# First attention: causal masks on VectorE and GpSimd instead of as matrix products, with a new order of work

## The reference

```python
qkv = x @ Wqkv.T + bqkv                       # x normalised over its 256 values before
q, k, v = split(qkv)                          # 16 heads of 16
q = q * rope + rotate(q) * (1.0 - rope)       # same for k
att = einsum('bhtd,bhsd->bhts', q, k) / 4
att = softmax(where(tril, att, -inf), axis=-1)
y = einsum('bhts,bhsd->bhtd', att, v)
return y @ Wproj.T + bproj                    # added to x
```

## Time and profile before

| | us |
|---|---|
| three runs | 3191.21, 3200.32, 3200.8 (median 3200.32) |
| the profiled execution | 3190.54, its span 3188.8 |
| seven bodies of the first attention | 79.5 to 629.5 of the span |
| the last body | 629.5 to 705 |
| TensorE busy over the span | 2539.1 |
| VectorE, ScalarE, GpSimd busy | 1845.6, 1238.0, 983.2 |
| mean granted TensorE clock | 0.908 of 2.4 GHz |

### The profile page before, as it was taken

The page is one execution under the profiler, slowest core; times in us unless marked ns, Lnnn a source line. Parts: engine busy times, 40 slices in busy tenths (PEclk is TensorE's granted clock), DMA queues, the critical chain, the costliest instruction groups (busy, mean ns, idle before and its releaser), DMA issues. The chain is left out here.

```text
span 3188.8 us, 51896 instructions
## 1 busy us (share of the span) xinstructions
PE 2539.1 (80%) x18615; PEld 2207.7 (69%) x18615; DVE 1845.6 (58%) x3241; ACT 1238.0 (39%) x1845; POOL 983.2 (31%) x1102
## 2 busy tenths in 40 slices
PE   1988888885069999980368777785999999999999
PEld 1777667765068888880256666675788888888888
DVE  5455555545057777775597777744744544544543
ACT  0444444442034444441123333332444444444444
POOL 3444445401734444437244444451000000000000
PEclk9899999985589999995589999997999999999999
DMA  2000000003256666654354554423422222221321
GB/s 80 1 2 2 1 1 1 1 11 128 97 179 209 211 213 212 211 193 145 94 139 126 130 129 123 123 57 116 146 97 79 86 84 77 89 81 66 100 78 60
DMA packets 195231, 317.13 MB, mean 99 GB/s; under 512 B 28757, under 2 KB 103449, under 8 KB 195097
## 3 DMA queue, kind: packets, MB, share of 16 engines
q1 hardware_dynamic: 182856, 277.00, 28.9%
q0 software_dynamic: 12240, 38.28, 3.5%
HBM read 274.83 MB, written 40.37 MB: 99 GB/s over the span
## 5 line engine op out<-in xcount | busy, mean ns | idle before, releaser
L2015 DVE TENSOR_TENSOR e_h_lo<-e_h,e_h_hi 128x512 fp32r<-128x512 f32 x320 | 221.6, 692 | 481.2 <-ACT e_h_hi L2081 481.0
L2068 ACT ACTIVATE e_h<-e_h_ps,e_b 128x512 f32<-128x512 f32 x320 | 220.3, 688 | 491.7 <-PE e_h_ps L2132 461.1
L2146 PE MATMUL e_y_ps<-e_w_hi,e_h_hi 128*128 128x256 f32 x1280 | 366.3, 286 | 22.8 <-DVE e_h_lo L2015 22.7
L2146 PE MATMUL e_y_ps<-e_w_hi,e_h_lo 128*128 128x256 f32 x1280 | 361.7, 283 | 0.0
L2146 PE MATMUL e_y_ps<-e_w_lo,e_h_hi 128*128 128x256 f32 x1280 | 361.5, 282 | 0.0
L1028 POOL TENSOR_TENSOR e_w_lo<-e_w,e_w_hi 128x2048 fp32r<-128x2048 f32 x40 | 186.5, 4662 | 315.1 <-ACT e_w_hi L1108 315.1
L2146 PEld LDWEIGHTS e_y_ps<-e_w_hi,e_h_hi 128*128 128x128 f32 x1280 | 243.1, 190 | 54.5 <-DVE e_h_lo L2015 39.6
L2132 PE MATMUL e_h_ps<-e_yT_hi,e_w_hi 128*128 128x512 f32 x640 | 257.9, 403 | 2.5 <-DVE e_yT_lo L2001 2.5
L401 DVE TENSOR_REDUCE a_top<-a_ring 128x2 f32<-128x1024 f32 (+3 forms) x256 | 202.7, 819 | 90.2 <-PE a_ring L602 89.3
L2132 PE MATMUL e_h_ps<-e_yT_lo,e_w_hi 128*128 128x512 f32 x640 | 253.6, 396 | 0.0
L2132 PE MATMUL e_h_ps<-e_yT_hi,e_w_lo 128*128 128x512 f32 x640 | 253.1, 396 | 0.0
(11 more groups left out here) (364 smaller groups left out, 7078.1 us busy)
## 6 DMA issues: line engine op xcount, KB each, us to landing
e_w<-in_w SPq DMA_DIRECT2D x82, 1024.0 KB, 5.4
e_spread<-share_store SPq DMA_DIRECT2D x512, 128.0 KB, 2.9
a_keys<-rows_store SPq DMA_DIRECT2D x128, 256.0 KB, 5.1
a_queries<-rows_store SPq DMA_DIRECT2D x86, 256.0 KB, 4.5
a_running_hidden<-rows_store SPq DMA_DIRECT2D x42, 256.0 KB, 4.5
e_xs<-sorted_x SPq DMA_DIRECT2D x41, 256.0 KB, 4.9
sorted_x<-zeros POOLq DMA_DIRECT2D x10, 1024.0 KB, 16.9
sorted_y<-e_ys POOLq DMA_DIRECT2D x40, 256.0 KB, 4.8
```

The source lines that it names most:

```text
L2015: dve.tensor_tensor(h_parts[c % 2][1][:, :], h[:, c % 2, :], h_parts[c % 2][0][:, :], ALU.subtract).then_inc(h_lo.sem, h_lo.tick())
L2068: act.activation(h[:, c % 2, :], h_ps[c % 2][:, :], ACT.Silu, bias=b1[:, c:c + 1]).then_inc(h_ready.sem, h_ready.tick())
L2146: last = pe.matmul(y_ps[n][:, 0:D], h_parts[c % 2][a][:, n * P:(n + 1) * P], w2[b][:, c, :], start=False, stop=(c == CH - 1 and m == 2))
```

## The change

The first attention, and nothing else, is rewritten in these points:

- No mask products. The three constant tiles and 12 loads go; one row tile `mask_row` (zeros, then the triangle of -1e30) is loaded.
- The maximum of a part is taken for each head by a `tensor_tensor_reduce` on VectorE: scores plus `mask_row`, times -1, minimum over the row. It writes its elements into a bf16 tile `masked` and the negated maximum into `top`. Eight instructions a pair instead of four. The two writes into the stacked q become `tensor_tensor` operations.
- In "b" the exponential is taken of unmasked scores, and GpSimd sets to zero what lies past the diagonal, with an `affine_select` in place, three a pair. The values product waits for it (`probs_cut`). In `b1` the two blocks change places, so that the diagonals lie side by side.
- GpSimd's stacking is merged (8 instructions a tile instead of 13) and cut into `turn`, `stack_high`, `stack_low`, which stand between the selects of pairs 0 to 4 of the body before.
- The normalisation moves to ScalarE (`Identity` with scale 1/sigma and bias -mean/sigma), for sequence s+2 in body s.
- "v0" moves from before "m" to behind "b1", and "o" one step later, between "a1" and "b1".
- All eight bodies are written out, without the loop; at the phase's end its semaphores are cleared.

```diff
-        A_COUNT = (1, 3, 4)
-        B_TILES = ((0, 0),), ((1, 0), (3, 384)), ((2, 0),)
+        A_COUNT = (2, 6, 8)
+        B_TILES = ((0, 0),), ((3, 0), (1, P)), ((2, 0),)
-        STEP = (("qk", 3), ("a0", 2), ("b0", 0), ("v0", -1), ("m", 1), ("a1", 2), ("b1", 0), ("v1", -1), ("a2", 2),
-                ("v2", -1), ("b2", 0), ("v3", -1), ("h", -1), ("o", -1))
+        STEP = (("qk", 3), ("a0", 2), ("b0", 0), ("m", 1), ("a1", 2), ("o", -2), ("b1", 0), ("v0", -1), ("a2", 2),
+                ("v1", -1), ("b2", 0), ("v2", -1), ("v3", -1), ("h", -1))
-            body(0, 0, False, True)
-            with engine.Fori(0, (B - 2) // 2) as i:
-                body(i * 2 + 1, 1, True, True)
-                body(i * 2 + 2, 0, True, True)
-            body(B - 1, 1, True, False)
+            for s in range(B):
+                body(s, s % 2, s > 0, s < B - 1)
+        def turn(engine, n, turned, straight, step, s):
+            for e in range(2):
+                engine.tensor_tensor(pairs_of(turned[:, :])[:, :, :, :, e], pairs_of(qk[:, n])[:, :, :, :, 1 - e],
+                                     unrope[:, n, :, e:DH0:2].unsqueeze(2).broadcast_to([P, 2, H0, DH0 // 2]),
+                                     ALU.mult).then_inc(step.sem, step.tick())
+            engine.tensor_tensor(straight[:, :], qk[:, n], rope[:, n].unsqueeze(2).broadcast_to([P, 2, H0, DH0]),
+                                 ALU.mult).then_inc(step.sem, step.tick())
+        def stack_high(engine, n, m, turned, straight, step, s):
+            engine.wait_ge(step.sem, step.at(step.n, s))
+            engine.tensor_tensor(q_high, twice(straight[:, 0]), twice(turned[:, 0]), ALU.add).then_inc(step.sem, step.tick())
+            engine.tensor_tensor(k_high, twice(straight[:, 1]), twice(turned[:, 1]), ALU.add).then_inc(step.sem, step.tick())
+            engine.tensor_tensor(qk[:, n], straight[:, :], turned[:, :], ALU.add).then_inc(step.sem, step.tick())
+        def stack_low(engine, n, m, step, done, s):
+            engine.wait_ge(step.sem, step.at(step.n, s))
...
+            sp.dma_start(mask_row[:, S - P:S], t["causal"][0]).then_inc(loaded.sem, loaded.tick(16))
+            def cut_probs(s, r, i):
+                pool.wait_ge(probs_ready.sem, probs_ready.at(3 * r + i + 1, s))
+                tiles = len(B_TILES[i])
+                diag = probs[r % 3][:, :, B_AT[i]:B_AT[i] + tiles * P]
...
+                pool.affine_select(out=diag, in_=diag, pattern=rows, compare_op=ALU.is_ge, fill=0.0, base=0,
+                                   channel_multiplier=-1).then_inc(probs_cut.sem, probs_cut.tick())
             def body(s, m, before, more):
                 if more:
                     add_bias(s + 1)
-                    stack(s + 1, 1 - m, range(TB))
+                for r in range(PAIRS):
+                    for i in range(3):
+                        cut_probs(s, r, i)
+                        slot = 2 * r + i // 2
+                        if not more or i == 1:
+                            continue
+                        if slot in (2, 4, 6):
+                            stack_low(pool, slot // 2 - 1, 1 - m, turn_step, stacked, s + 1)
+                        if slot in (0, 2, 4, 6):
+                            turn_tile(s + 1, slot // 2)
+                        if slot in (1, 3, 5, 7):
+                            stack_high(pool, slot // 2, 1 - m, turned, straight, turn_step, s + 1)
+                        if slot == 8:
+                            stack_low(pool, TB - 1, 1 - m, turn_step, stacked, s + 1)
...
-                            dve.reduce_max(top[r % 2][:, tb, :], banks(k)[:, :, at:at + (tb + 1) * P],
-                                           AX.X).then_inc(top_taken.sem, top_taken.tick())
+                            for j in range(2):
+                                wide = (tb + 1) * P
+                                if top_taken.n >= 2:
+                                    dve.wait_ge(top_taken.sem, top_taken.at(top_taken.n - 1))
+                                dve.tensor_tensor_reduce(masked[j][:, 0:wide], banks(k)[:, j, at:at + wide],
+                                                         mask_row[:, S - wide:S], -1.0, -2 * NEG, ALU.add, ALU.min,
+                                                         top[r % 2][:, tb, j:j + 1]).then_inc(top_taken.sem, top_taken.tick())
-                        dve.tensor_scalar(at[:, :, :, 0], top[r % 2][:, :, :], -1.0, None, ALU.mult).then_inc(top_negated.sem,
+                        dve.tensor_tensor(at[:, :, :, 0], top[r % 2][:, :, :], top[r % 2][:, :, :],
+                                          ALU.min).then_inc(top_negated.sem, top_negated.tick())
-                        dve.scalar_tensor_tensor(out=at[:, :, :, 1], in0=top[r % 2][:, :, :], scalar=-1.0,
+                        dve.tensor_tensor(at[:, :, :, 1], top[r % 2][:, :, :], at[:, :, :, 0],
+                                          ALU.subtract).then_inc(max_ready.sem, max_ready.tick())
+            def norm(s):
+                act.wait_ge(stat_step.sem, stat_step.at(CENTRED))
+                if s:
+                    act.wait_ge(xT_done.sem, xT_done.at(KC, s - 1))
+                for n in range(TB):
+                    at = s * TB + n
+                    act.activation(xn[:, n, :], g.x[:, at, :], ACT.Identity, bias=centre[:, at:at + 1],
+                                   scale=rstd[:, at:at + 1]).then_inc(xn_ready.sem, xn_ready.tick())
...
-                            for u, cut in ((0, slice(0, P)), (1, slice(HALF, P))):
-                                for j in range(2):
-                                    rows = slice(j * HALF, (j + 1) * HALF)
-                                    last = pe.matmul(banks(k)[:, j, diag + cut.start:diag + cut.stop], half_eye[rows, u, :],
-                                                     mask_ts[rows, u, cut], start=False, stop=(u == 1))
...
-                            pe.wait_ge(probs_ready.sem, probs_ready.at(3 * (r + 1), s))
+                            pe.wait_ge(probs_cut.sem, probs_cut.at(3 * (r + 1), s))
```

More of the change, by code:

```diff
@@ L109, in attention0_phase @@
         HALF = P // 2
-        half_eye = sb("half_eye", [P, 2, P], F32R)
-        mask_ts = sb("mask_ts", [P, 2, P], F32R)
-        mask_st = sb("mask_st", [P, 2, P], F32R)
+        mask_row = sb("mask_row", [P, S])
+        masked = [sb(f"masked{k}", [P, S], BF16) for k in range(2)]
         ident_r = sb("ident_r", [P, P], F32R)
-        stats, mv = sb("stats", [P, NT, 6]), sb("mv", [P, NT, 2])
-        var, rstd, newton, half, ones = (sb(n_, [P, NT]) for n_ in ("var", "rstd", "newton", "half", "ones"))
+        mv, rstd, centre = sb("mv", [P, NT, 2]), sb("rstd", [P, NT]), sb("centre", [P, NT])
         xn = sb("xn", [P, TB, D])
@@ L142, in attention0_phase @@
         w_raw = probs[0][:, :, :].rearrange("p j c -> p (j c)")[:, 0:KC * W3].rearrange("p (c n) -> p c n", c=KC)
+        stats = probs[2][:, 1, 0:NT * 6].rearrange("p (n k) -> p n k", n=NT)
+        var, newton, half, ones = (probs[2][:, 0, k * NT:(k + 1) * NT] for k in range(4))
         wp_raw = probs[1][:, 0, 0:KC * D].rearrange("p (c n) -> p c n", c=KC)
-        const_raw = probs[2][:, 0, 0:6 * P].rearrange("p (m u q) -> p m u q", m=3, u=2)
         ring = [ps(f"ring{k}", (P, 2 * S)) for k in range(3)]
@@ L161, in attention0_phase @@
         ORDER = []
-        for step in range(-3, PAIRS + 1):
+        for step in range(-3, PAIRS + 2):
             for what, ahead in STEP:
@@ L282, in prepare @@
                 add_bias(0)
-                stack(0, 0, range(TB // 2))
+                for n in range(TB // 2):
+                    turn_tile(0, n)
+                    stack_high(pool, n, 0, turned, straight, turn_step, 0)
+                    stack_low(pool, n, 0, turn_step, stacked, 0)
                 pool.wait_ge(stat_step.sem, stat_step.at(PREPARED))
@@ L470, in body, with prepare @@
                         act.activation(heads_T[:, :], pO[:, :], ACT.Copy).then_inc(heads_out.sem, heads_out.tick())
-            turns(act, lambda: high_parts(0, 0), body, lambda: high_att(B - 1, 0))
+                        if r == 1 and s + 2 < B:
+                            norm(s + 2)
+            def prepare():
+                norm(0)
+                high_parts(0, 0)
+                norm(1)
+            turns(act, prepare, body, lambda: high_att(B - 1, 0))
         @block.tensor
```

103 lines of the change are left out of this document (37 added, 66 removed).

## The result

The changed kernel took 3252.9 us (median of four, 3242.1 to 3257.6), the kernel before on the same chip 3198.9: ratio 1.0186, interval 1.0159 to 1.0213. The forecast was 3180 with a range to 3240, so both direction and range failed. The profiled execution took 3257.3 us, its span is 3255.2.

The account below looks back on a forecast made before the run. TensorE was taken to bound the kernel before, GpSimd's queue the changed turns. Seven turns -5, start -5 and last turn -10 sum to -20 us: from the median 3200.3 to 3180, range 3110 to 3240.

Parts of the forecast that it names:

- the two small operations behind the maxima: VectorE's two writes into the stacked q after the maxima: 1 us each beside GpSimd, lower end 0.17, upper 1.28.
- The longest wait at the values product: TensorE's values product of pair 3 stands 7 to 12 us in each turn, behind a select on GpSimd.
- GpSimd's queue, the turn of 75.6: GpSimd's stacking, now behind the first select, delays TensorE in pair 3: a turn takes 75.6 us against 78.6.
- The selects: Three a pair on GpSimd, of 256, 512 and 256 columns: 1.95 us a pair, range 0.4 to 4.0.
- Rival A: GpSimd's queue is dearer and delays the values product of pair 3: slower, about 3235 at the upper price; 17%.
- rule of 4 us at pair 3: Each microsecond more a pair of selects delays pair 3's values product 4 us and the turn nearly 5.
- the other sum in the prediction: Selects on GpSimd at line rate and 1.2 GHz: 0.85 us for 1024 columns, some 2 us a turn lower.
- The hand schedule: A turn of the first attention laid out pair by pair, without the new limit on GpSimd: 63 us.
- rival D: GpSimd is not in the way; TensorE or VectorE bounds at 63 to 66 us a turn: 3095; 15%.
- The clock: TensorE's clock falls after the rest of 7 to 12 us in each turn: 2.3 us more a turn.
- Rival B: TensorE stays at 1.2 GHz behind the wait: +7 a turn makes 3213, with no last-turn gain 3223; 17%.
- Last turn and start: Last turn, with nothing to stack: -10 us (bounds -16 and +4). Start, with fewer loads and merged stacking: -5 us.

## Why the prediction was wrong, step by step

**The step that failed: the two small operations behind the maxima.** The prediction priced them at 1 us each beside GpSimd, "up to the 1.28 us of one long GpSimd instruction". It read an instruction's wait as ending at the next boundary on the other engine, because the one row it had, 0.65 us at 362.73, ended so. Most did: pairs of 1.3 and 1.2 us stand in nearly every turn. But one a turn ran on for 9.7 to 12.7 us, across eleven to fourteen boundaries. The bound was wrong in kind: it should have been what is left of GpSimd's unbroken row, and that row was itself worked out in the prediction (35.8 us), for another purpose. Its longest measured 24.5 us in the changed kernel, and 38.5 without the small operations. What had kept the operations harmless showed in the trace of before and was not read: GpSimd's own rests, which leave no row over 4.1 us. Two of them, in that kernel:

```profile
359.75 0.72 POOL L217 TENSOR_TENSOR a_straight<-a_qk,a_rope 128x256 f32<-128x256 f32 x1
360.55 1.42 POOL L221 TENSOR_TENSOR a_q_stack<-a_straight,a_turned 128x256 fp32r<-128x256 f32 x2
...
363.31 1.26 POOL L226 TENSOR_TENSOR a_qk<-a_straight,a_turned 128x512 f32<-128x512 f32 x1
364.65 0.74 POOL L228 TENSOR_TENSOR a_q_stack<-a_qk,a_q_stack 128x256 fp32r<-128x256 f32 x1
```

Between L217's end (360.47) and L221 lie 0.08 us, and again between L226 and L228: a piece waits there for its predecessor's result. The change puts selects between such pieces, so the waits are fulfilled when they are reached and the rests vanish. The prediction counted this as "about a microsecond of waits on itself", a cost. Putting three such rests a turn back takes the long stalls away (1.0186 to 1.0036). They do it by keeping the rows short: in the kernel before, too, most small operations that began beside GpSimd left at an ordinary boundary, and only 16 of 66 in a rest.

**Size of the failure.** Against the two repairs that leave all work in place (1.0018 and 1.0036) it is worth 1.5 to 1.7%, 48 to 54 us, of the loss of 1.9%. With the operations gone altogether it is 2.3% (0.9955), which takes away their ordinary cost too. That kernel is 13.5 us below the kernel before on its chip (3175.9 for 3189.4), where 20 were forecast with 1 us for each of them. The stall itself is about 10 us a turn, of which TensorE stood 7.6 to 11.4.

**The longest wait at the values product.** It was forecast at 7 to 12 us in pair 3; in the changed kernel the longest there is 2.1. TensorE came to it late. In the kernel without the small operations the wait is there, at pair 3, but 3.5 us.

**GpSimd's queue, the turn of 75.6.** Right in kind, and masked. With the small operations gone the turn is 75.0. That the chain is the bound there is shown: half of it moved early makes the turn 71.6. That the two numbers lie so close is luck. In that kernel GpSimd's first select is 24.9 us behind the turn's start (20.1 in the prediction), its selects are cheaper than priced, and so the last select of pair 3 ends at 56.9 (55.9); TensorE comes to it at 53.4 and not at 49, and waits 3.5 us and not 7. With the operations kept and a pause behind each select a turn is about 78 us, hardly shorter than before (78.6).

**Prices.** Each as measured, with what the prediction took. The selects, 2 x 0.411 + 0.643 = 1.47 us a pair (1.95 taken, range 0.4 to 4.0). The maxima, 2 x (0.686 + 0.553 + 0.419 + 0.286 + 4 x 0.083) = 4.55 (4.5 taken). The merged turn, 0.86 a piece in place of 0.74. Three of the prediction's own figures do not follow from its rows. The selects' upper end by the scan's 3.3 ns a column is 3.4 us for 1024 columns, not 4.0. Rival A was priced without the 2.3 us a turn for the clock: with it the turn is even with before at about 2.1 us a pair, not 2.6, and the whole kernel at about 2.5, not 3.0. And selects at 0.85 in place of 1.95 us a pair would by its rule of 4 us at pair 3 take over 4 us off a turn, not 2.

For the selects the other sum in the prediction, by one-input operations at line rate in the Trainium skill (GPSIMD Engine Reference, "Engine selection"), gave 0.85 us for the columns: the measured 1.47 lies nearly midway. Its rate itself fits the step from 256 to 512 columns for the select (0.23 us for the 256 more; an estimate from the 1.2 GHz of that page of the Trainium skill is 0.21), not for the multiplication (0.64).

**The hand schedule.** It gave 63 us a turn without GpSimd. The nearest kernels have 69 to 73, at clocks of 0.86 to 0.93, so TensorE's own side was some 8 us too low, and rival D's 3095 was out of reach: without selects and small operations 3134 was had.

**The clock.** Forecast: below 0.85 in the seven turns would mean that something else is wrong. It was 0.71 to 0.81, and it was a follower, mostly: the same matmuls ran at 0.89 (144 to 594 us) with the small operations gone. Rival B, the clock as a cause of its own, is not excluded for the rest: with pauses behind the selects and no long stall it is 0.84 (147 to 536), and the turn is 78 us and not 75; the small operations' ordinary time and the clock were not told apart there. The kernel with the normalisation on VectorE speaks for a part of the clock's own: no small operations, shorter waits for the selects, and yet 77 us a turn at 0.82.

**Last turn and start.** The last turn: -5.5 (-10 forecast). VectorE's first operation begins at 20.59 in place of 24.32, -3.7 as forecast, and TensorE's first transposes of the turns at 74.30 in place of 78.46, -4.2 (-5).

**The sum.** -5 for the start and about -5 for the last turn came; the seven turns came at +66 in place of -5.

## What to carry to other kernels

Before an engine's queue is repacked, look at what rests in it serve somebody else: a small VectorE operation between SBUF tiles, on TensorE's path, should be bounded by what is left of GpSimd's unbroken row, not by one instruction of it, once such rows are 10 us and more. Cheapest cures, in order of what they gave here: have the result written where it is needed by the instruction that makes it; place the row where its owner is idle; put one wait on its own result into the row. And a wait per block is worth writing when the producer works per block.

## What was not expected of the hardware

- A VectorE operation of 8 elements a partition stood for 9.7 to 14.2 us while GpSimd went through its row, with one operand or two, and ended 0.03 us behind the row's last instruction. In the two kernels with waits of 0.08 us put into the row none took over 1.34 us.
- Not every one stands so long. Of the 522 that began beside GpSimd in the nine kernels with the operations and without multiplications, under 9 us into its row, none took over 1.34 us; they left at the next boundary or the one behind it, most with no rest there (1.33 us at 270.69). Of the 34 that began later in a row 29 stood to its end, whatever GpSimd ran when they began: low parts, L214 (191.56 above) or L226. Why the place in the row decides, and why five left early, stays open.
- A multiplication in place on GpSimd let the small operations in while it ran; a select did not.
- Accumulator reads of 83 ns and the maxima with one operand in PSUM never stood: the longest of 512 reads took 86 ns, the longest maximum of 512 columns 694 ns, in every kernel alike.
- On GpSimd the select in place took 0.41 us for 256 columns and 0.64 for 512, a multiplication by a constant over the same elements 0.85 and 1.49.
